# Moving the last block of similarity scores behind the first probability transposes, and the output statistics behind the first VectorE eviction of the second transposes, in a fused cross-attention and expert kernel

## The reference, cut to what matters

```
x1 = x + tanh(g_xattn) * LN_out(softmax(q k^T / 8) v Wout)     # q = LN(x) Wq: 16 heads of 64; k, v: 77 context rows and one null row
x2 = LN(x1)
out = x1 + tanh(g_ffn) * (shared(x2) + sum over the top 8 of 32 experts of w_e * expert_e(x2))
```

## Time and profile before

| | |
|---|---|
| median of 3 runs | 2084.86 us (2079.21 to 2086.57) |
| the profiled execution | 2083.68 us, its span 2082.0 us |
| PE busy | 1982.1 us (95%) |
| PE weight loads | 1754.7 us (84%) |
| DVE busy | 1610.9 us (77%) |
| ACT busy | 1378.0 us (66%) |
| POOL busy | 1180.3 us (57%) |
| mean granted clock of TensorE | 0.978 of full speed |

### The profile page before, as it was taken

How to read it: one execution, slowest core, us unless ns; L and a number is a source line. 1 busy time by engine, 2 the same in 40 slices (tenths; PEclk the granted TensorE clock), 3 DMA queues, 4 the chain that set the end, 5 groups by cost and what they waited for, 6 DMA issues and landing times. The chain is left out here.

```text
span 2082.0 us, 44128 instructions
## 1 busy us (share of the span) xinstructions
PE 1982.1 (95%) x14690; PEld 1754.7 (84%) x14690; DVE 1610.9 (77%) x3769; ACT 1378.0 (66%) x3991; POOL 1180.3 (57%) x1286
## 2 busy tenths in 40 slices
PE   7999799999999999999997799999999999999995
PEld 7898688888888888888876688888888888888884
DVE  3432258888888888888886776669999999999996
ACT  3211177788777887777763277778777777777771
POOL 1322104777777777777776300027777777777775
PEclk9999899999999999999988899999999999999997
DMA  8654478767666666666668999999999999999998
GB/s 270 222 190 165 144 296 316 274 240 243 234 244 239 239 240 238 240 237 239 239 240 260 378 298 286 285 313 391 402 398 391 396 391 396 393 399 390 397 362 286
DMA packets 299750, 614.15 MB, mean 295 GB/s; under 512 B 55397, under 2 KB 167750, under 8 KB 299526
## 3 DMA queue, kind: packets, MB, share of 16 engines
q1 hardware_dynamic: 250374, 477.05, 64.5%
q0 software_dynamic: 49152, 134.28, 17.5%
HBM read 305.13 MB, written 306.05 MB: 294 GB/s over the span
## 5 line engine op out<-in xcount | busy, mean ns | idle before, releaser
L1653 POOL DMA_INDIRECT parts<-results_dram,kept_index x512 | 518.7, 1013 | 383.9 <-DMA results_dram<-y 220.0
L837 POOL DMA_INDIRECT pages_dram<-rows,kept_index x512 | 529.6, 1034 | 198.8 <-issue 143.2
L895 ACT ACTIVATE exps<-sim,minus_max 128x78 f32<-128x78 f32 x1024 | 316.1, 349 | 14.7 <-DVE minus_max L988 14.7
L1674 ACT ACTIVATE w_h<-w_raw 128x768 fp32r<-128x768 f32 x159 | 134.1, 843 | 158.7 <-DMA w_raw<-in_experts 157.9
L895 ACT ACTIVATION_READ_ACCUMULATOR exps<-sim,minus_max 128x1 f32 x1024 | 236.2, 231 | 0.0
L1762 DVE SCALAR_TENSOR_TENSOR parts<-parts,kept_weight 128x256 f32<-128x256 f32 x448 | 213.4, 476 | 1.6 <-DMA parts<-dense_dram 0.5
L1859 PE MATMUL xps<-ident,xin 128*128 128x128 f32 x1272 | 167.1, 275 | 19.2 <-DVE wq_l L1724 7.7
L1736 DVE TENSOR_TENSOR w_l<-w_raw,w_h 128x768 fp32r<-128x768 f32 x159 | 151.6, 954 | 41.8 <-ACT w_h L1674 41.7
L141 PE MATMUL yps<-w_h,hid_h 128*128 128x256 f32 x636 | 179.6, 282 | 1.5 <-DVE hid_l L1819 1.0
L143 PE MATMUL yps<-w_l,hid_h 128*128 128x256 f32 x636 | 178.5, 281 | 0.0
L142 PE MATMUL yps<-w_h,hid_l 128*128 128x256 f32 x636 | 178.3, 280 | 0.0
(11 more groups left out here) (243 smaller groups left out, 6026.3 us busy)
## 6 DMA issues: line engine op xcount, KB each, us to landing
xin<-pages_dram SPq DMA_DIRECT2D x159, 512.0 KB, 10.9
results_dram<-y SPq DMA_DIRECT2D x159, 512.0 KB, 9.7
w_raw<-in_experts SPq DMA_DIRECT2D x159, 385.0 KB, 10.0
pages_dram<-blank SPq DMA_DIRECT2D x108, 512.0 KB
pages_dram<-blank SPq DMA_DIRECT2D x12, 1536.0 KB
keys_dram<-keys SPq DMA_DIRECT2D x16, 624.0 KB, 4.4
kT<-keys_dram SPq DMA_DIRECT2D x32, 312.0 KB
v<-values_dram SPq DMA_DIRECT2D x32, 308.0 KB
```

The source lines that it names most:

```text
L837: pool.indirect_dma_start(dram["pages"], bass.IndirectOffsetOnAxis(ap=kept_index[:, at:at + 1].bitcast(U32), axis=0), buffer(batch)[:, k / ...
L895: last = act.activation(exps[u % 2][:, h, :], scores(u)[:, h // 4, h % 4, :], ACT.Exp, bias=minus_max[u][:, h:h + 1], accum_out=row_sum[u] ...
L1653: pool.indirect_dma_start(parts[slot(batch, t)][:, k, :], None, done, bass.IndirectOffsetOnAxis(ap=kept_index[:, at:at + 1].bitcast(U32), ...
```

## The change

Two things are moved, and nothing is added or removed. On TensorE `similarity(3, b)` stands behind the transposes T0a instead of directly behind `similarity(2, b)`, and so between T0a and Ob. On VectorE `statistics(1, ...)` stands behind the eviction of T0b instead of ahead of it (T0a is not evicted by VectorE, so its place in the list was directly ahead of T0b).

```diff
@@ vector, step @@
-                if name == "T0a" and 1 <= b <= B:
+                if name == "T0b" and 1 <= b <= B:
                     dve.wait_ge(ring_full, nth(RING, "Ob", b))
                     statistics(1, lambda t: bank("Ob", b)[:, t * D:(t + 1) * D], b - 1)
@@ tensor, step @@
                 output(name, b, par, h)
                 if name == "Oa" and here:
                     similarity(2, b)
+                if name == "T0a" and here:
                     similarity(3, b)
```

## The result

The changed kernel took 2093.06 us (median of 15 runs, 2088.03 to 2114.15), the kernel before, run alongside, 2083.05 us (15 runs, 2079.21 to 2086.95). The ratio is 1.0052, with an interval of 1.0037 to 1.0067: 10 us slower. The forecast was 2089 in a range of 2076 to 2102. The profiled execution took 2093.06 us, its span is 2091.3 us, the mean granted clock 0.977.

The account below looks back on a forecast made before the run. TensorE's queue was taken to bound the attention phase, 26.02 us a step. The terms -8.7 + 7.7 + 6.8 = +5.8 us on the profiled 2083.68 us gave 2089.5, taken as 2089, range 2076 to 2102.

Parts of the forecast that it names:

- The wait for `pT`: TensorE, T1a to Q0: the wait for VectorE's copy of T0b goes, 0.28 us a step, 8.7 us in all.
- The logits next: VectorE: logits come later, at 580.2 + 0.24 instead of 579.60; a slack of 0.3 us before T1b hides it.
- The fourth rival: TensorE at T1b: logits free their bank too late, 0.2 us wait a step, 2095 us; chance 0.10.
- The switches: TensorE, between 64-row scores and 128-row matmuls: second entry and exit cost 0.24 us a step, 7.7 us in all.
- the second rival: TensorE: switches are free, the scores cost nothing or gain 0.11 us a step, 2073 us; chance 0.11.
- GpSimd's queue: GpSimd to ScalarE to TensorE: `shift` 1.3 us later, Oa 0.4 us late in 17 steps, cost 6.8 us.
- The first rival: GpSimd's delay reaches only ScalarE, N2 always hides behind Oa's wait, 2083 us; chance 0.22.
- The third: `make_rstd(2)`'s delay holds the step at N2, all steps late or slipping further, 2094 to 2110 us; chance 0.17.
- The other door: TensorE, `similarity(3)`: its 0.11 us wait for unit 1's exponentials goes; their 0.35 to 0.9 us delay falls into ScalarE's waits.
- The expert phase ... keeps its length in the sum: After the attention phase: starts when that ends, length unchanged; 2 or 3 us either way estimated from run to run.
- the sum of 5.8 us: Whole kernel: -8.7 for the `pT` wait, +7.7 for the moved scores, +6.8 for the late `shift`.
- a sign of being wrong: Oa never moves, steps are shorter than 25.8 us, or the expert phase changes by more than 3 us.

Follow-up runs that it names:

- the run with `shift` early and the statistics moved: Kernel before with statistics behind the copy of T0b and `make_rstd(2)` one scatter earlier, scores not moved: 2073.87 us against 2082.25, ratio 0.9958.
- both units behind T0a: Kernel before with statistics behind the copy of T0b, `make_rstd(2)` one scatter earlier, `similarity(2)` and `similarity(3)` behind T0a: 2077.59 us against 2080.94, ratio 0.9983.

## Why the prediction was right, and where not

**The wait for `pT`.** Right. T1a to Q0 fell from 0.62 to 0.39 us, 0.04 less of a gain than the 0.27 forecast (the 0.35 us expected for what is left was not reached); the run with `shift` early and the statistics moved shows it as 26.03 - 25.77 = 0.26 us a step.

**The logits next.** Right in the steady state: the logits start 14.0 us into a step (14.49 in the late one shown, less 0.45) instead of 13.3, as forecast, and T1b did not wait. The fourth rival falls there. It holds in the last step alone, where no Q0 stands between T1a and T1b: the wait of T1b for the logits grew from 0.38 to 0.89 us. The prediction did not ask about that step.

**The switches.** Right to 0.01 us: 2.88 us forecast, 2.88 found; 0.24 us a step alone. The sum over the nearest rows held although the trace had neither of the two switches, and the second rival falls: with the switches free it would have been less than the 2.64 of before, not more. Of the two rules of the Trainium skill weighed there, the one of TensorEngine Tiling (Array Packing), Key Properties, that a change of the tiling mode drains the engine, agrees with these numbers.

**GpSimd's queue.** Right in each link: `var_eps` 14.66 us into a step that was late by 0.45 at Oa, so 14.2 (forecast 14.1), `shift` 1.30 and 1.90 (1.4 and 1.95), N2 at 2.63 and 3.23 (2.6 and 3.1), Oa 0.45 us late (0.4). The number of late steps was 14 in one execution and 19 in the other (17). The first rival, that it is absorbed, falls: taking the delay away from the changed kernel gives steps of 26.01 us. The third, that every step is late or slips by another slot, did not come either: `shift` never came later than 1.91 us into a step.

**The other door.** Missed, though it did not cost in the changed kernel. The prediction took `similarity(3)`'s wait for the exponentials of unit 1 as 0.11 us that goes, and did not ask what it would be with `shift` late: 0.35 us more in every step, as the run with the statistics alone shows. I had the delay of the exponentials (0.35 to 0.9 us) in the text, and let it "fall into waits that ScalarE has anyway".

**"The expert phase ... keeps its length in the sum".** This is the term that failed: it was put at nothing, and the sum of 5.8 us is too small against the 10 measured. The steps alone grew by 4.9 us in one profile and by 7.1 in the other, on both sides of the 5.8. What was missing lies outside them. Between the last attention step and the first page 2.7 and 2.8 us were lost, so this part isn't the chance that the prediction allowed for: it comes again with the kernel. Behind the first page 1.2 us were lost in the one and 1.9 gained in the other, and 0.6 and 0.7 us were lost ahead of the second step; such differences stand between two executions of one kernel too (1.3 us at the second step with the statistics and the early `shift`, 2.4 behind the first page with both units behind T0a). Counted from the start of the last attention step to the end, the loss is 3.8 us in the first profile and 0.9 in the second, and the first of these is beyond the 3 us that the prediction named as a sign of being wrong. The time came within the range because the sum over the steps was close, in spite of this term.

## What to carry to other kernels

On an engine that is always busy, a step moved by a microsecond on another engine matters by what is queued behind its reader, not by its reader: follow the queue (here statistics, then eight scatters, then `shift`, then `apply_rows`, then two units of exponentials) to the next wait of the busy engine, in all its variants. A wait taken away at one place often comes back at the next; try each pair of edits together, since here each of the two edits alone made it slower (1.0031 and 1.0042), and with `make_rstd(2)` and `key` moved as well the two together pay (0.9936). Don't put matmuls of half the rows between full ones without need: a switch to and fro cost 0.24 us here. And ask what a step at the edge of the pipeline, where some work is left out, does to the slack that hides a delay.

## What the runs showed of the hardware

The granted clock at the end of a phase can depend on the kernel in a repeatable way: over 40 us it was 0.74 in both profiles of the changed kernel and 0.91 in both of the kernel with the statistics moved and `shift` early, for work that is nearly the same. The time to the first page differs by some 5 us between them (129.5 against 124.0), as much as the late steps cost. That the clock is its whole cause was not shown, and three profiles speak against a simple rule: with the statistics alone moved the clock was 0.87 and the page still came at 128.4 us, and the kernel before, with 0.79, had it at 126.8 where the changed one had 129.5, after the same 42 us at the lower level.

One and the same scatter in GpSimd's queue took either 1.06 or 1.66 us, nothing between, from step to step, and this 0.6 us alone decided which steps were late. In the kernel before it took the longer time in 17 of 28 steps; with the statistics alone moved in one.
